# Small prologue loads issued by SyncE instead of ScalarE, and the residual slots released ahead of ScalarE's blanks

## The reference, cut to what matters

```
scores = x @ w + b                      # one number per token
idx = top_k(scores, 179)                # 0.7 of 256
h = take x at idx                       # (16, 179, 192)
h = h + attn0(layernorm(h))             # additive attention: tanh(q_t + k_s) . ws + bs, 12 heads of 16
h = h + ffn0(layernorm(h))              # 192 -> 768 -> 192, weights and activations fake-quantized
h = h + attn1(layernorm(h))             # dot-product attention, integer softmax
h = h + ffn1(layernorm(h))              # 16 experts, one per token by argmax
```

## Time and profile before

| | us |
|---|---|
| median of three runs | 1312.71 (1312.66 to 1315.25) |
| profiled execution, its own time | 1311.38 |
| its span in the trace | 1309.3 |
| mean granted TensorE clock | 0.981 |

### The profile page before, as it was taken

The page is one execution under the profiler, slowest core; times in us unless marked ns, Lnnn a source line. Parts: engine busy times, 40 slices in busy tenths (PEclk is TensorE's granted clock), DMA queues, the critical chain, the costliest instruction groups (busy, mean ns, idle before and its releaser), DMA issues. The chain is left out here.

```text
span 1309.3 us, 44013 instructions
## 1 busy us (share of the span) xinstructions
PE 1075.0 (82%) x18818; PEld 816.7 (62%) x18821; DVE 1075.5 (82%) x2086; ACT 1003.9 (77%) x962; POOL 859.1 (66%) x931
## 2 busy tenths in 40 slices
PE   2867877877877888787788877899799999998796
PEld 1554655655655566565556655799466777676595
DVE  6989999899999999999999998577666777878342
ACT  3389999899999999999999999588345555543242
POOL 2079889798898888889888889775001233334354
PEclk9989999999999999999999999999899999999798
DMA  7999999700000000000000000110000200002451
GB/s 186 350 361 358 355 342 335 257 11 10 11 2 10 11 3 11 10 9 4 11 10 3 11 10 2 51 24 1 2 4 3 66 19 17 17 20 60 122 154 51
DMA packets 78546, 107.83 MB, mean 82 GB/s; under 512 B 6963, under 2 KB 76489, under 8 KB 78356
## 3 DMA queue, kind: packets, MB, share of 16 engines
q1 hardware_dynamic: 66138, 90.93, 21.3%
q0 software_dynamic: 5360, 8.02, 1.9%
q10 hardware_dynamic: 6860, 6.12, 1.7%
HBM read 18.32 MB, written 83.85 MB: 78 GB/s over the span
## 5 line engine op out<-in xcount | busy, mean ns | idle before, releaser
L1002 ACT ACTIVATE work<-work 128x2864 f32<-128x2864 f32 (+1 forms) x272 | 707.7, 2726 | 9.9 <-DVE work L446 9.0
L446 POOL TENSOR_TENSOR work<-shared 128x1253 f32<-128x1253 f32 (+1 forms) x272 | 612.9, 2267 | 92.2 <-PE psum L1991 80.1
L1991 PE MATMUL psum<-work,ws_place 128*32 128x179 f32 x8640 | 393.9, 320 | 152.9 <-ACT work L1002 142.0
L446 DVE TENSOR_TENSOR work<-psum,shared 128x1611 f32<-128x1611 f32 (+3 forms) x288 | 488.0, 1722 | 0.7 <-PE psum L1991 0.2
L1991 PEld LDWEIGHTS psum<-work,ws_place 128*32 128x32 f32 x8640 | 263.1, 110 | 251.8 <-ACT work L1002 193.2
L991 ACT ACTIVATE pt_region<-psum,bs_neg 128x384 f32<-128x384 f32 x144 | 103.4, 719 | 2.5 <-PE psum L2003 2.5
L2191 PE MATMUL psum<-shared 32*32 32x179 f32 (+1 forms) x3456 | 99.1, 326 | 1.2 <-DVE peaks L1647 0.7
L1375 DVE SCALAR_TENSOR_TENSOR p_sb<-psum,bs_col,s_top 128x358 f32<-128x358 f32 x144 | 82.1, 570 | 14.9
L877 POOL DMA_INDIRECT xs_dram<-w_store,slot_i x24 | 28.5, 1189 | 83.3 <-DVE slot_i L1747 76.6
L1372 DVE TENSOR_REDUCE s_top<-psum 128x2 f32<-128x358 f32 x144 | 71.6, 498 | 7.9 <-PE psum L1991 6.8
L2003 PE MATMUL psum<-ident,p_sb 128*128 128x128 f32 x416 | 77.2, 293 | 0.0
(11 more groups left out here) (419 smaller groups left out, 2001.7 us busy)
## 6 DMA issues: line engine op xcount, KB each, us to landing
xs_dram<-pad_row SPq DMA_DIRECT2D x23, 3088.0 KB, 28.2
pt_region<-xs_dram ACTq DMA_DIRECT2D x19, 193.0 KB, 2.7
pt_region<-xs_dram SPq DMA_DIRECT2D x19, 193.0 KB, 2.8
xs_dram<-pad_row SPq DMA_DIRECT2D x1, 2895.0 KB, 26.8
pt_region<-v_sb SPq DMA_DIRECT2D x22, 96.0 KB
work<-in_x SPq DMA_DIRECT2D x2, 768.0 KB, 9.9
work<-in_x ACTq DMA_DIRECT2D x2, 768.0 KB, 12.7
work<-in_L_ffn_W2T SPq DMA_DIRECT2D x1, 1536.0 KB
```

The source lines that it names most:

```text
L446: ins = eng.tensor_tensor(dst[:, a * KEEP:e * KEEP].rearrange("p (u s) -> p u s", s=KEEP), k[:, h * KP:h * KP + KEEP].unsqueeze(1).to_broa ...
L1002: act.activation(a, a, ACT.Tanh).then_inc(tanh_done, 1)
L1991: ins = pe.matmul(bank_s[p % 2][32 * quad:32 * quad + 32, at:at + KEEP], ws_place[:, j, :], arg_slot(n)[:, u * KEEP:(u + 1) * KEEP], start ...
```

## The change

ACT no longer waits for the token chunks and no longer issues the 27 DMAs; SP issues them, in the same order, behind its layer 0 ffn loads and ahead of the layer 1 loads. SP has already waited for all token chunks there; the wait for `w0_blank` moves with the DMAs. ACT's wait for `filled` and `resid_blank` and the addition of 2 to `resid_ready` move from behind the DMAs to ahead of the wait for `consts` and of the blanks.

```diff
--- before.py
+++ after.py
@@ -513,6 +513,24 @@
             sp.dma_start(s_gelu[:, :], I["L0_ffn_s_gelu"].partition_broadcast(128)).then_inc(wf_loaded, 16)
             sp.dma_start(s_out[:, :], I["L0_ffn_s_out"].partition_broadcast(128)).then_inc(wf_loaded, 16)
 
+            sd = small_loaded
+            sp.dma_start(bs_col[:, :], I["L0_attn_bs"].partition_broadcast(128)).then_inc(sd, 16)
+            for h in range(8):
+                sp.dma_start(ws_col[HD * h:HD * h + HD, :], I["L0_attn_ws"].rearrange("(d o) -> d o", o=1)).then_inc(sd, 16)
+            w = w0_loaded
+            sp.wait_ge(w0_blank, 1)
+            for dst, wt, bias in ((wq0, "L0_attn_WqT", "L0_attn_bq"), (wk0, "L0_attn_WkT", "L0_attn_bk")):
+                for r, (lo, hi) in enumerate(((0, DA), (DA, D))):
+                    sp.dma_start(dst[0:hi - lo, r, 0:D], I[wt][lo:hi, :]).then_inc(w, 16)
+                    sp.dma_start(dst[0:hi - lo, r, D:WIDE], I[wt][lo:hi, DA:D]).then_inc(w, 16)
+                row = I[bias].rearrange("(o d) -> o d", o=1)
+                sp.dma_start(dst[DB:DB + 1, 1, 0:D], row).then_inc(w, 16)
+                sp.dma_start(dst[DB:DB + 1, 1, D:WIDE], row[:, DA:D]).then_inc(w, 16)
+            for dst, wt, bias in ((wv0, "L0_attn_WvT", "L0_attn_bv"), (wo0, "L0_attn_WoT", "L0_attn_bo")):
+                sp.dma_start(dst[:, 0, :], I[wt][0:DA, :]).then_inc(w, 16)
+                sp.dma_start(dst[0:DB, 1, :], I[wt][DA:D, :]).then_inc(w, 16)
+                sp.dma_start(dst[DB:DB + 1, 1, :], I[bias].rearrange("(o d) -> o d", o=1)).then_inc(w, 16)
+
             for n, name in enumerate("qkv"):
                 sp.dma_start(wsrc[n][0][:, :], I[f"L1_attn_W{name}"][0:DA, :]).then_inc(w1_loaded, 16)
                 for h in range(2):
@@ -911,13 +929,16 @@
 
         @block.scalar
         def _(act):
-            sd = small_loaded
             act.dma_start(tok_w[:, :], I["L0_tok_w"].rearrange("d o -> (d o)").partition_broadcast(128)).then_inc(tok_loaded, 16)
             act.dma_start(tok_b[:, :], I["L0_tok_b"].partition_broadcast(128)).then_inc(tok_loaded, 16)
             xv = I["x"].rearrange("b (t p) d -> p (b t) d", p=128)
             for n in (1, 3):
                 act.dma_start(x_all[:, 8 * n:8 * n + 8, :], xv[:, 8 * n:8 * n + 8, :]).then_inc(x_loaded[n], 16)
+
             act.preload_act_table_set("exp_and_others")
+            act.wait_ge(filled, 1)
+            act.wait_ge(resid_blank, 1)
+            act.sem_inc(resid_ready, 2)
             act.wait_ge(consts, 1)
 
             def blank(part):
@@ -932,29 +953,6 @@
             for part in v_extra:
                 for n in range(2):
                     ins = blank(part[:, n, :, :].rearrange("p h v -> p (h v)"))
-            for n in (1, 3):
-                act.wait_ge(x_loaded[n], 16)
-            act.dma_start(bs_col[:, :], I["L0_attn_bs"].partition_broadcast(128)).then_inc(sd, 16)
-            for h in range(8):
-                act.dma_start(ws_col[HD * h:HD * h + HD, :], I["L0_attn_ws"].rearrange("(d o) -> d o", o=1)).then_inc(sd, 16)
-            w = w0_loaded
-            act.wait_ge(w0_blank, 1)
-            for dst, wt, bias in ((wq0, "L0_attn_WqT", "L0_attn_bq"), (wk0, "L0_attn_WkT", "L0_attn_bk")):
-                for r, (lo, hi) in enumerate(((0, DA), (DA, D))):
-                    act.dma_start(dst[0:hi - lo, r, 0:D], I[wt][lo:hi, :]).then_inc(w, 16)
-                    act.dma_start(dst[0:hi - lo, r, D:WIDE], I[wt][lo:hi, DA:D]).then_inc(w, 16)
-                row = I[bias].rearrange("(o d) -> o d", o=1)
-                act.dma_start(dst[DB:DB + 1, 1, 0:D], row).then_inc(w, 16)
-                act.dma_start(dst[DB:DB + 1, 1, D:WIDE], row[:, DA:D]).then_inc(w, 16)
-            for dst, wt, bias in ((wv0, "L0_attn_WvT", "L0_attn_bv"), (wo0, "L0_attn_WoT", "L0_attn_bo")):
-                act.dma_start(dst[:, 0, :], I[wt][0:DA, :]).then_inc(w, 16)
-                act.dma_start(dst[0:DB, 1, :], I[wt][DA:D, :]).then_inc(w, 16)
-                act.dma_start(dst[DB:DB + 1, 1, :], I[bias].rearrange("(o d) -> o d", o=1)).then_inc(w, 16)
-
-
-            act.wait_ge(filled, 1)
-            act.wait_ge(resid_blank, 1)
-            act.sem_inc(resid_ready, 2)
 
             def pick_move(b):
```

## The result

Five executions of the changed kernel took 1300.38 to 1308.56 us, median **1303.68**, against 1312.71 for the kernel before (1311.96 to 1315.26): ratio 0.9929, 95% interval [0.9913, 0.9945]. The forecast was 1305.6, range 1300.5 to 1310. The profiled execution is the slowest of the five: 1308.56, its span 1306.8. So its total says 2.8 us where the median says 9.0, and each stage has to be compared by itself.

A forecast was written before the change was run, and what follows sets the result against it. The prediction took ACT's DMA issuing ahead of the release to bound the first picks; -7.80 for the picks and +0.7 for the fills gave -7.1, from 1312.71 to 1305.6 us, range 1300.5 to 1310.

The forecast's parts named there:

- ACT's issuing is the bound, and the one-hot is next: First picks: PE waits for the release behind ACT's 27 DMA issues; without them DVE's one-hot at 21.48 sets pick(0).
- The main term: Start of pick(0) on PE: 21.55 instead of 29.35 once the release comes early, a gain of 7.80 us.
- The block shift: All picks on PE move earlier together by the gain at pick(0), with at most 0.5 us more.
- DVE catches up: DVE's one-hots for the picks: choose(2) at 25.90, 1.07 us late, then 1.78 per round, so the lateness does not grow.
- ACT's blanks, the nine small loads, the 18 weights: nothing: Later blanks on ACT and loads moved to SP's queue delay nobody; cost nil, the weights with 11 us of margin.
- The fills under the attention: +0.7: Attention beside SP's fills: the common stretch grows from 180 to some 201 us, costing 0.7 us by density of stalls.
- the one given 0.72: Forecast case for the whole kernel's time: 1303 to 1308 us, chance 0.72.
- The sentence on instruction fetch: Skill's statement for PE under the fills: blocks arrive by DMA, crossings mostly hidden; by it the fills term is nil, time 1304.9.
- The stalls thin out: Rival: PE's stalls under the fills thin out or vanish; 1299.2 at the end, case 1299 to 1303, chance 0.12.
- more stalls eat the gain: Rival: PE's instructions come late under the fills in three or more batches; 1312.4 to 1318.1; slower 0.04, no change shares 0.08.
- the release does not open the picks: Rival: PE really waited for something else before the first pick; 1312.7, within the 0.08 for no change.
- DVE is not caught up: Rival: in the picks only DVE's idle time of 6.73 us is gained; 1306.7, inside the forecast's own range.

The follow-up runs named there:

- e7: The changed kernel with SP's 24 fills paced, two behind each batch's v_ready instead of all in one go; median 1302.09 us.
- e8: e7 with PE kept warm by identity products, 32 behind the last pick and 24 behind the first projections; median 1299.47 us, ratio 0.9901.
- e10: e9 with PE kept warm by identity products, 24 behind the last pick and 22 behind the first projections; median 1304.94 us, ratio 0.9932.
- e11: e9 with the fills paced and PE kept warm by identity products; median 1299.37 us, ratio 0.9894.
- e1: The changed kernel run again without any edit; median 1302.20 us, ratio 0.9918.
- e3: The changed kernel with the release put back behind ACT's blanks, the 27 DMAs staying on SP; median 1300.80 us, ratio 0.9895.
- e9: e3 run once more, the 27 DMAs on SP and the release behind the blanks; median 1301.67 us, ratio 0.9912.
- e2: The kernel before with only the release moved ahead of the blanks, the 27 DMAs left on ACT; median 1308.62 us, ratio 0.9959.

## Why the prediction was right, and where it was off

- *ACT's issuing is the bound, and the one-hot is next.* Right, and shown by parts: with 18 DMAs left pick(0) is at 24.73, with none at 21.3 to 21.8. In the profile after, pick(0) starts 0.06 behind the one-hot (20.62 + 0.66 = 21.28), 21.34 for a forecast of 21.55; the tokens had landed 0.2 earlier.
- *The main term, 7.80, was sized too small.* At pick(0) it is 8.01 in the first pair of profiles, and 8.5 between the means of the three profiles with all 27 DMAs on ACT and the eight with none there. ACT's 27 issues take 13.2 to 14.0 us from one execution to the next, and the profile of before held the short end; in the profile after the one-hot was also 0.2 earlier.
- *The block shift.* At the last pick the first pair has 8.56, not 8.01, since the second pick took 2.12 before and 1.68 after. It looks as if the standstill had made it slow, but the other profiles do not bear this out. With the standstill the second pick took 1.79 to 2.81, without it 1.68 in four profiles and 2.32 to 2.63 in four (e7, e8, e10, e11). From pick(0) to the last pick it was 26.5 to 27.5 us with all 27 DMAs on ACT and 26.3 to 27.4 with none. The first picks are slow in every profile, and so are the score rows ahead of the standstill: four products take 1.12 at 20.30 and 0.63 later in the same kernel. What ends it is the granted clock: its records begin in each profile with a rise to 1.00 within the first two picks (33.35 before, 23.78 after), and at that time the products' spacing falls from 0.32 to 0.16. Earlier there is no record, and the windows print 1.00 there for want of one; that PE had the lower level is inferred from the spacing. The rise comes 3.3 to 5.5 us after the start of pick(0) with all 27 DMAs on ACT and 2.2 to 5.2 with none, so the two overlap. The shift as a block was right on the average, and the 0.5 us on top in the first pair was mostly the draw of that rise.
- *DVE catches up.* Right: choose(2) at 25.61 (25.90 forecast), a pace of 1.77, no wait before the last.
- *ACT's blanks, the nine small loads, the 18 weights: nothing.* Right. Blanks from 8.63 to 17.27, the first pick move at 24.21; the last weight issued by 32.0 (34.2 forecast), PE's wait for it not in the waits. On SP the 27 cost 12.6 us, 0.47 each, where 13.2 to 14.6 were expected, and the fills started at 44.5 to 45.9 and not at 46.7.
- *The fills under the attention: +0.7.* The mechanism was right, the size and for most executions the sign were not. The excess was 8.2 in the profile after and 1.1, 1.3 and 0.9 in the three other profiles of kernels with the same fills, against 5.8 and 3.9 before. A density, excess per microsecond of overlap, was the wrong model: the gaps belong to a few fixed places of PE's program, and their length is drawn anew. One of the rows that the term was built on, the 2.30 us ahead of 194.85, was moreover a wait for DVE; the gap "issue" of that batch is the 0.63 at 187.60. The two highest of eleven times of the changed kernel are 1308.56 and 1308.61. The first is the profiled one and shows the excess of 8.2; for the second there is no profile. Whether the mean excess fell with the change can't be told from two profiles on one side and four on the other; the medians of the later jobs (11.4 below before, where the last pick gives 8.6) leave room for some 2 us of it. There was luck in the time forecast: a main term 0.7 too small and a fills term of +0.7 that most executions do not show err the same way. The medians of e1, e3 and e9, 1300.80 to 1302.20, lie in the case that had been given 0.12 (1299 to 1303), and only the first median, 1303.68, in the one given 0.72.
- *The sentence on instruction fetch.* I had weighed the Trainium skill's Runtime: NRT & Kernel Launch, Instruction fetch mechanics, against the gaps. Its first half, that instructions arrive in blocks by a DMA queue, agrees with the 148 packets of 16 KB and with gaps at fixed counts of instructions. Its second half, that crossing a block is mostly hidden, holds by number: of some 148 packets, 2 to 5 leave a gap in attention 0. But beside an unbroken stream of 3 MB writes a gap took up to 3.46 us and the excess reached 8.2, so the term was not nil in each execution.
- *Rivals.* "The stalls thin out" came true in e1, e3 and e9; "more stalls eat the gain" in the profiled execution, partly; "the release does not open the picks" and "DVE is not caught up" are excluded by the rows. That the release alone would open only pick(0) and pick(1), since ACT's own pick move stands behind the DMAs too, was not among my rivals, and is what makes the moved DMAs the part that matters.

## What to carry to other kernels

A DMA issue costs the issuing engine about half a microsecond, and everything behind it in that queue pays: put small loads on a queue that nobody waits for, and look not only for the semaphore that is released late but also for the next task of the same engine. Look at the granted clock behind a standstill too: here 2.9 us of waiting made two picks 2.8 us longer (e2). And before a term is priced from one profile, take a second profile of the same kernel: here two executions of it differed by 0.7 us in the stall that the change removes, by 2 in the stalls under the fills, and by 2 in a stage that nothing had touched.

## What the runs showed of the hardware

- PE's program has fixed places, by the count of instructions, at which it can stand still for its next block of instructions: 0.16 to 3.46 us beside an unbroken stream of about 360 GB/s. It goes on 1.2 to 1.6 us behind the end of a 16 KB packet of the `instruction` queue. With the stream paced to a mean of 120 to 160 GB/s the gaps were at most 1.13 or missing. Adding instructions ahead moves them to other work.
- Not each gap "issue" is of this kind: all thirteen profiles have two of 0.98 to 0.99 in the second attention (967 and 984 in the kernel before), with next to no DMA traffic, at the same instruction whatever was put ahead. What they are is open.
- Standstills of PE of 5.9 us (ahead of the projections) and of 2.9 (e2) were followed by a stretch at 0.50. Ahead of the projections it lasted about 7 us in some executions and 10 in others, and with it the lag from last pick to first tanh was 18.9 to 20.4; it was 17.4 to 18.2 with the warm products.
- From the first picks on PE's products are spaced 0.32 us, then 0.16 from the first recorded rise of the granted clock on. That rise came 2.2 to 5.5 us after the start of pick(0), differently in each execution, with the standstill ahead of it or without.
- A small DMA issue cost 0.49 to 0.52 us on ACT, beside SP's own issues, and 0.47 on SP, where ACT issued none. Whether the small difference comes from the engine or from issuing side by side is not told apart.
